# Maxima of the first head's scores: two groups of keys in one VectorE pass, by way of the positive part of their difference

## The reference

```
x = x + L0_xattn(layernorm(x), ctx)      # one head of width 128
x = x + L0_ffn(layernorm(x))             # 8 experts, top 1
x = x + L1_xattn(layernorm(x), ctx)      # 8 heads of width 64, softmax over 6,404 keys
x = x + L1_ffn(layernorm(x))             # 32 experts, top 4 within 4 of 8 groups

# L1_xattn
q = x @ Wq;  k = ctx @ Wk;  v = ctx @ Wv           # 8 heads of 64
attn = softmax(q k^T * 64**-0.5);  out = attn v;  out @ Wo + bo
```

## Time and profile before

| | |
|---|---|
| median of 3 runs | 1416.0 us (1412.88 to 1417.68) |
| the profiled execution | 1413.19 us, of it 1411.4 us span |
| PE / DVE / ACT / POOL busy | 1365.8 / 1017.1 / 803.0 / 969.5 us |
| the first head's maxima, first product to last reduction | 279.64 to 341.42 us of the span |
| first scores of the main loop | 346.65 us |
| granted clock of TensorE from 296.8 to 344.5 us | 0.50 |

### The profile page before, as it was taken

One profiled execution on the slowest core, in us unless ns is written; L12 is line 12 of the kernel. 1 busy time (PEld: TensorE's weight loads), 2 busy tenths in 40 slices (PEclk: granted clock), 3 DMA queues, 4 the chain that ended last, 5 costly groups with the idle time before them and its releaser, 6 DMA issues.

```text
span 1411.4 us, 20075 instructions
## 1 busy us (share of the span) xinstructions
PE 1365.8 (97%) x6259; PEld 786.0 (56%) x6259; DVE 1017.1 (72%) x1420; ACT 803.0 (57%) x1599; POOL 969.5 (69%) x562
## 2 busy tenths in 40 slices
PE   5989998889999999999999999999999999999998
PEld 3877776524455555555545555555555555556665
DVE  8976656598887677777777767677767675876555
ACT  3458887422566656666556665655665655554432
POOL 5001112342889999999999999899999999986110
PEclk9999999976999999999999999999999999999999
DMA  6640000310000200200020020002002000000011
GB/s 175 206 132 18 18 16 10 77 22 0 1 1 1 51 8 1 51 9 0 1 58 1 1 50 9 1 0 59 1 1 48 8 1 1 8 1 24 25 40 36
DMA packets 80537, 41.38 MB, mean 29 GB/s; under 512 B 64301, under 2 KB 72254, under 8 KB 80166
## 3 DMA queue, kind: packets, MB, share of 16 engines
q1 hardware_dynamic: 80454, 40.28, 11.4%
HBM read 26.53 MB, written 13.74 MB: 29 GB/s over the span
## 4 chain that ended last, share of the span: by engine, by line
PE 89%; DVE 6%; DMA 3%; ACT 1%; issue 1%; POOL 0%; SPq 0%; ACTq 0%; POOLq 0%; DVEq 0%
PE ps L1537 26%; PE ps L1524 15%; PE ps L1525 13%; PE ps L1484 9%; PE ps L1471 3%; DMA v_scratch<-v_stage 3%; DVE chunk_max L1054 2%; PE ps L1713 2%; PE ps L1344 2%; PE ps L1345 2%; PE ps L1346 2%; PE ps L1335 2%; PE ps L1333 2%; PE ps L1334 2%; PE ps L1699 1%; PE ps L1701 1%
## 5 line engine op out<-in xcount | busy, mean ns | idle before, releaser
L605 POOL TENSOR_TENSOR psums<-psums,probs 126x1024 f32<-126x1024 f32 (+1 forms) x392 | 821.4, 2095 | 66.0 <-ACT probs L811 11.0
L1054 DVE TENSOR_REDUCE chunk_max<-ps 128x2 f32<-128x1008 f32 (+1 forms) x416 | 473.3, 1182 | 154.2 <-PE ps L1484 153.8
L811 ACT ACTIVATE probs<-ps 126x512 f32<-126x512 f32 (+1 forms) x816 | 412.8, 623 | 270.0 <-PE ps L1525 261.9
L1537 PE MATMUL ps<-probs,v_mem 126*64 126x512 f32 (+1 forms) x1632 | 389.8, 598 | 0.0
L1524 PE MATMUL ps<-q_heads,ring 128*126 128x512 f32 (+1 forms) x816 | 334.2, 410 | 0.6
L1525 PE MATMUL ps<-q_low,ring 128*126 128x512 f32 (+1 forms) x816 | 321.3, 394 | 0.0
L1537 PEld LDWEIGHTS ps<-probs,v_mem 126*64 126x64 f32 (+1 forms) x1632 | 111.6, 136 | 173.4 <-issue 123.0
L1117 DVE TENSOR_TENSOR xn<-xn,probs 126x512 f32<-126x512 f32 x126 | 181.4, 1440 | 21.9 <-ACT probs L811 16.4
L1524 PEld LDWEIGHTS ps<-q_heads,ring 128*126 128x126 f32 (+1 forms) x816 | 151.2, 185 | 80.7 <-issue 44.1
L755 ACT CAST ring<-ps 64x252 fp32r<-64x252 f32 (+1 forms) x356 | 128.3, 360 | 117.3 <-PE ps L1471 114.2
L1484 PE MATMUL ps<-ring,q_heads 64*128 64x504 f32 (+1 forms) x416 | 163.7, 468 | 11.1 <-DVE chunk_max L1054 9.0
(11 more groups left out here) (227 smaller groups left out, 1410.9 us busy)
## 6 DMA issues: line engine op xcount, KB each, us to landing
v_scratch<-v_stage SPq DMA_DIRECT2D x51, 252.0 KB
v_mem<-v_scratch SPq DMA_DIRECT2D x8, 1606.5 KB
ctx_mem<-in_ctx_t SPq DMA_DIRECT2D x3, 803.2 KB, 8.3
vslot<-in_ctx_rows SPq DMA_DIRECT2D x51, 47.2 KB
pair_w<-in_f_pairs SPq DMA_DIRECT2D x17, 128.0 KB, 2.2
xn<-rden_scratch SPq DMA_DIRECT2D x14, 128.0 KB
pair_w<-in_f_pairs SPq DMA_DIRECT2D x17, 65.0 KB, 1.9
x_tok<-in_x SPq DMA_DIRECT2D x1, 512.0 KB, 4.2
```

The costliest lines, as they stand in the source:

```text
L605: pool.tensor_tensor(sums[0:r, 0:width], sums[0:r, 0:width], probs[0:r, n % PROBS, 0:width], ALU.add).then_inc(c_sum, 1)
L811: act.activation(probs[0:r, n % PROBS, cols(half)], ps[0:r, score_bank(t, half), :], ACT.Exp, scale=float(HD) ** -0.5).then_inc(c_exped, 1)
L1054: dve.tensor_reduce(chunk_max[:, h % 2, i:i + 2, c], ps[:, banks[0]:banks[1] + 1, 0:group_tiles(c) * KT], AX, ALU.max).then_inc(c_reduced, 1)
L1537: ins = pe.matmul(ps[half * HD:(half + 1) * HD, B_ACC, :], v_tiles[0:r, h % 2, t, :], probs[0:r, n % PROBS, cols(half)], start=(t == 0), s ...
```

## The change

For two groups of keys with scores a and b, max(a, b) = max(a - b, 0) + b. The first 12 groups are taken two at a time. One such double step `n` (24 in all) covers two groups and two query tiles:

- TensorE accumulates a - b in the two banks of a first pair: two matmuls with the queries on the first group, and two with the negated queries `q_neg` on the second. It puts b alone into a second pair, with two more matmuls. That is six matmuls of 504 columns where two steps had four.
- ScalarE applies Relu to the first pair, 128 x 1008 elements, into a buffer `beyond` (two slots, in memory of `probs` that is not yet in use).
- VectorE runs two `tensor_tensor_reduce`, one for each query tile: 504 elements of b from a bank plus 504 elements of the buffer, and the maximum of the sums into `chunk_max`.

The 13th group keeps the old form: four single steps. So the loop has 28 turns where it had 52. The three pairs of banks are shared out anew: a - b of turn n waits for VectorE's turn n - 2, and b of turn n waits for ScalarE's turn n - 1. The key projections go to ten turns listed in `KEYS_AT`, the second head's queries to turns 16 and 21. `q_neg` is made by VectorE ahead of `q_lo`. The idle matmuls of this stage and of the first lines of the main loop are gone. `row_maxima` of the first head reads 7 columns of `chunk_max` per query tile where it read 13. Semaphores `max_found` and `max_row` are merged into `c_found` and `c_row`.

```diff
+STEPS = TT // 2
+TWO_STEPS = GROUPS_H // 2 * STEPS
+FIRST_STEPS = TWO_STEPS + STEPS
+KEYS_AT = (3, 6, 8, 10, 13, 15, 18, 20, 22, 24)
+QUERIES_FIRST = (16, 21)
...
+        beyond = probs[:, 2:6, 0:GT * KT].rearrange("p (s b) k -> p s b k", s=2)
+        q_neg = q_heads[:, 2, :]
...
@@ ScalarE
-            for g in range(EARLY[2], AHEAD):
-                k_first(g)
-                if g in (EARLY[2] + 1, EARLY[2] + 2):
-                    q_hi(1, g - EARLY[2] - 1, B_AUX)
+            for n in range(FIRST_STEPS):
+                if n < TWO_STEPS:
+                    first = FIRST_PAIRS[2 * n % 3][0]
+                    act.wait_ge(c_max, 4 * n + 2)
+                    if n >= 2:
+                        act.wait_ge(c_reduced, 2 * n - 2)
+                    act.activation(beyond[:, n % 2], ps[:, first:first + 2, 0:GT * KT], ACT.Relu).then_inc(c_over, 1)
+                if n in KEYS_AT:
+                    k_first(EARLY[2] + KEYS_AT.index(n))
+                if n in QUERIES_FIRST:
+                    q_hi(1, QUERIES_FIRST.index(n), B_AUX)
...
@@ VectorE
+            def first_maxima(n):
+                dve.wait_ge(c_max, 4 * n + 4 if n < TWO_STEPS else 2 * (n + TWO_STEPS) + 2)
+                c, i = 2 * (n // STEPS), 2 * (n % STEPS)
+                if n >= TWO_STEPS:
+                    first = FIRST_PAIRS[(n + TWO_STEPS) % 3][0]
+                    dve.tensor_reduce(chunk_max[:, 0, i:i + 2, c], ps[:, first:first + 2, 0:group_tiles(c) * KT], AX,
+                                      ALU.max).then_inc(c_reduced, 1)
+                else:
+                    dve.wait_ge(c_over, n + 1)
+                    for half in range(2):
+                        extra = beyond[:, n % 2, half, :]
+                        dve.tensor_tensor_reduce(out=extra, in0=ps[:, FIRST_PAIRS[(2 * n + 1) % 3][half], 0:GT * KT], in1=extra,
+                                                 scale=1.0, scalar=LOWEST, op0=ALU.add, op1=ALU.max,
+                                                 accum_out=chunk_max[:, 0, i + half, c:c + 1]).then_inc(c_reduced, 1)
+
+            for half in range(2):
+                dve.wait_ge(c_qhi, half + 1)
+                dve.tensor_scalar(q_neg[:, cols(half)], ps[:, FIRST_PAIRS[2][half], :], -1.0, None, ALU.mult).then_inc(c_neg, 1)
...
@@ TensorE
-                if step >= GROUPS_H * STEPS - 6:
-                    pe.wait_ge(c_kfull, AHEAD)
-                    idle(1, FIRST_KP)
-            idle(5, FIRST_KP)
+            first_q = q_heads[:, 0, :], q_low[:, 0, :]
+            for n in range(FIRST_STEPS):
+                c, i = 2 * (n // STEPS), 2 * (n % STEPS)
+                if n < TWO_STEPS:
+                    banks = FIRST_PAIRS[2 * n % 3]
+                    if n == 1:
+                        pe.wait_ge(c_qlo, 2)
+                    if n >= 2:
+                        pe.wait_ge(c_reduced, 2 * n - 2)
+                    first_products(c, i, banks, first_q, True, False)
+                    if n < 2 * STEPS:
+                        pe.wait_ge(c_neg, 1 + i // STEPS)
+                    first_products(c + 1, i, banks, (q_neg, q_neg), False, True)
+                    if n:
+                        pe.wait_ge(c_over, n)
+                    first_products(c + 1, i, FIRST_PAIRS[(2 * n + 1) % 3], first_q, True, True)
+                else:
+                    if n == TWO_STEPS + 1:
+                        pe.wait_ge(c_over, TWO_STEPS)
+                    else:
+                        pe.wait_ge(c_reduced, 2 * TWO_STEPS + {0: -2, 2: 0, 3: 1}[n - TWO_STEPS])
+                    first_products(c, i, FIRST_PAIRS[(n + TWO_STEPS) % 3], first_q, True, True)
...
             row_shift(0, B_AUX)
-            idle(3, FIRST_KP)
+            pe.wait_ge(c_kfull, AHEAD)
...
                         if k and h == 0 and b == 0:
-                            idle(3, B_KEYS)
                             pe.wait_ge(c_shift, 2)
```

More of the change, by code:

```diff
@@ L59 @@
 FIRST_PAIRS, FIRST_KP = ((0, 1), (2, 3), (6, 7)), 4
+GT = 4
+GROUPS_H = -(-TILES // GT)
+STEPS = TT // 2
[3 more added lines that the diff above has]
+QUERIES_FIRST = (16, 21)
+LOWEST = -3.0e38
 EARLY = (3, 3, 5)
 B_LOGITS, B_HIDDEN, B_SPREAD, B_MASK = 0, (1, 2, 3, 6), (5, 1, 2, 3), (7, 0)
[L67 to L68 removed]
 RING = 16
 AHEAD = RING - 1
[L71 removed]
 PROBS = 2 * GT
@@ L1099, in add_last_output @@
                 ins.then_inc(c_x, 1)
+            def first_maxima(n):
[15 more added lines that the diff above has]
+                dve.tensor_scalar(q_neg[:, cols(half)], ps[:, FIRST_PAIRS[2][half], :], -1.0, None, ALU.mult).then_inc(c_neg, 1)
             for half in range(2):
                 q_lo(0, half, FIRST_PAIRS[2][half])
[L1103 to L1106, removed]
+            for n in range(FIRST_STEPS):
+                first_maxima(n)
+                if n in QUERIES_FIRST:
+                    q_lo(1, QUERIES_FIRST.index(n), B_AUX)
             row_maxima(0, GROUPS_H * STEPS)
@@ L1576, in _ @@
                 q_proj(0, half, FIRST_PAIRS[2][half])
[L1577 to L1585, removed]
-                if step % STEPS == 1 and early < AHEAD:
-                    k_proj(early)
-                    early += 1
-                if step in (STEPS + 2, 2 * STEPS + 2):
-                    half = step // STEPS - 1
+            pe.wait_ge(ring_rows, 1)
@@ new lines, in _, with first_products @@
+            pe.wait_ge(c_qhi, 2)
+            pe.wait_ge(c_qlow, 1)
+            def first_products(c, i, banks, q_rows, start, stop):
+                pe.wait_ge(c_khi, c + 1)
+                for half, q in enumerate(q_rows):
+                    rows = slice(half * HD, (half + 1) * HD)
+                    ins = pe.matmul(ps[:, banks[half], 0:group_tiles(c) * KT], q[rows, tile_cols(i + half)],
+                                    ring[rows, c % RING, 0:group_tiles(c), 0, :], start=start, stop=stop)
+                    if stop:
+                        ins.then_inc(c_max, 1)
@@ new lines, in _ @@
+            first_q = q_heads[:, 0, :], q_low[:, 0, :]
+            for n in range(FIRST_STEPS):
+                c, i = 2 * (n // STEPS), 2 * (n % STEPS)
[18 more added lines that the diff above has]
+                    first_products(c, i, FIRST_PAIRS[(n + TWO_STEPS) % 3], first_q, True, True)
+                if n in KEYS_AT:
+                    k_proj(EARLY[2] + KEYS_AT.index(n))
+                if n in QUERIES_FIRST:
+                    half = QUERIES_FIRST.index(n)
```

18 lines of the change are left out of this document (10 added, 8 removed).

## The result

The changed kernel takes **1403.45 us** (median of 4 runs, 1401.96 to 1406.81), where the kernel before, beside it, takes 1415.57 (1412.88 to 1417.68). The ratio is 0.9919, 95% interval 0.9894 to 0.9943: faster, by 12.1 us in the medians where -7.3 was forecast. The profiled execution is the longest of the four: 1406.81 us, span 1405.0. I read both profiles, since they differ by 5.7 us in the same code.

What follows compares the result with a forecast made beforehand. VectorE was taken to bound the first head's maxima stage. Stage -9.4, gap -2.4, main loop's clock +2.0 and stage's clock +2.5 sum to -7.3 us, forecast 1409 us from the median 1416.0, range 1403.5 to 1418.5.

Steps and rivals of the forecast that it cites:

- likeliest case: Whole kernel: clock mostly up, 0.6 to 0.8 us per new VectorE instruction, 1405.5 to 1411.5 us; chance 0.50.
- The stage: First head's maxima: ends at 332.0 instead of 341.42 us, -9.4 at full clock, with +2.5 for spells at 0.50.
- The new VectorE instruction: In each double turn: tensor_tensor_reduce of 504 elements takes 0.70 us, bounds 0.60 and 1.14, so 1.40 a turn.
- the ring: In the double turns: waits through TensorE, ScalarE and VectorE set the pace, 3.55 us for two turns, no engine full.
- The key turns: Ten turns with a key projection: ScalarE's copies make the next Relu 0.475 us late.
- The clock in the stage: First head's maxima: spells at clock 0.50, a fifth of the 12.4 us that a whole stage there costs, +2.5 us.
- The gap: From last reduction to main loop's first scores: 2.83 us instead of 5.23 as the idle matmuls go, -2.4 us.
- The main loop at 0.50: Main loop's start: without the idle matmuls it begins at clock 0.50, costing 1.7 to 3.4 us, taken as +2.0.
- The clock stays up: Rival on TensorE's clock: both clock terms are nothing, -11.8 us, 1404; chance 0.08.
- The clock falls early and stays low: Rival on the stage's clock: at 0.50 from 296.7 us or at once, -1.3 to +2.7 us, 1415 to 1419; chance 0.20.
- Two instructions: Rival on the new VectorE instruction: main pass plus a short one of 0.26, 0.96 us each, -2.1, 1414; chance 0.08.
- As dear as the reduction: Rival on the new VectorE instruction: 1.14 us for 504 elements, +2.7, or likelier +8.1 at clock 0.50, 1424; chance 0.12.

Runs made afterwards that it cites:

- a2: The changed kernel run again, unaltered; 1401.86 us, ratio 0.9927 to the kernel before.
- e5: Kernel of e1 with two idle matmuls more in each of the first 16 turns without a key projection; 1401.39 us, ratio 0.9924.
- e6: Changed kernel with the second copy of each key projection moved from ScalarE to VectorE; 1402.0 us, ratio 0.9934.
- e4: Changed kernel with each turn's Relu split into two instructions, one per bank, with their own signals; 1400.92 us, ratio 0.9918.
- e9: Kernel of e5 with the additional VectorE instruction of e3 in each double turn; 1403.73 us, ratio 0.9925.
- e1: Changed kernel with the idle matmuls of before put back at the stage's end and the main loop's start; 1402.17 us, ratio 0.9916.
- e7: Kernel before with two idle matmuls more behind the products in most steps of the stage; 1436.15 us, ratio 1.0174.
- e8: Kernel before with one or two idle matmuls ahead of the products of every step of the stage; 1412.88 us, ratio 0.9999.
- e3: Changed kernel with one more VectorE instruction, its result unused, in each of the 24 double turns; 1411.08 us, ratio 0.9979.
- e2: Kernel before without the idle matmuls at the stage's end and the main loop's start; 1411.08 us, ratio 0.9988.
- c1: Kernel of e5 plus e4's Relu halves, e6's copy and one idle matmul ahead of the products of the last four turns; 1397.04 us, ratio 0.9878.

## Why the prediction was right, and where its sizes were off

**Direction and bound: right.** The stage was VectorE's, it is shorter by 8.9 and 10.5 us, and that arrives in the total one for one: the rest differs from before by +0.3 and -0.8 us. Forecast 1409 (1403.5 to 1418.5), measured 1403.45, 0.05 below the end of the range and outside the likeliest case's own (1405.5 to 1411.5). From the ratio and the median shown before it is 0.9919 x 1416.0 = 1404.5, just inside. Against a2's profile (-13.4) the forecast of -7.3 was 6.1 us off: 1.9 in the stage at full clock, 1.7 in the clock of the stage, 2.8 in the rest, and -0.3 in the gap.

**The stage: -9.4 + 2.5 = -6.9 forecast, -8.9 and -10.5 measured.** At full clock 52.4 us were forecast, and e5 took 50.5 (2.9 us of it at 0.50, in the last reductions, which kept their spacing).
- *The new VectorE instruction*, 0.70 taken, is the largest of the terms that were mis-sized, 0.11 of the 0.25 us by which the ring was too long. It takes 0.605 from start to start, the lower bound of 0.60. The nearest row was of a plain two-input instruction at 0.69 for 512 elements, a duration of one; it was taken for a spacing. Here the duration is 0.68 too, and the spacing is not.
- *Relu*, 1.05 taken, takes 1.01. The prediction's own walk with 1.29 for VectorE's turn and 1.01 gives 51.2 us, 1.2 of the 1.9 that it was off. Single steps of 0.86 in place of 0.95 are 0.4 of the rest. The remaining 0.3 has no sum of its own, but the hand-overs and products of the ring were 0.10 too long.
- *The key turns*, +0.475 each: two turns with a key took 3.85 against 3.30, so 0.55. Near in size, and right in that the copies delay the next Relu (e6). But the path was not ScalarE's work alone, as the prediction had it: it runs through the key projection too, for which ScalarE waits.
- *The clock in the stage*, +2.5: between e5 and the two profiles it is +2.4 (15.3 us at 0.50) and +0.8 (3.5 us). Right for the profiled execution, too much for most. "Spells rather than 45 us on end" is what came.

**The ring of waits: shown.** e4 shortened a latency and no work, and got 0.43 of 0.42 us. e9 added work to VectorE, paid 2.4 us for 10.4, and its ring adds up too. The forecast of an even turn of 1.775 was wrong in form, as two turns run back to back and then wait; the ring sets what two of them take. And it sets only the pairs without a key projection; the others have the ring of 3.85.

**The gap: -2.4 forecast, -2.1 measured.** Right.

**The main loop at 0.50: +2.0 forecast, +0.3 in the balance.** The main loop did start at 0.50 for 5.5 us, and e1 says that costs up to 2.6, so the term itself was right. The prediction forgot that the rest of the kernel before isn't free of such spells: it had 6.8 us at 0.50 near 1324 us, and the profiled change 3.4 us there. That varies from run to run, and it may well be what hid the term: the rest of the kernel before is 1064.8 us, while e7 and e8, the same code behind the stage with no such spell, have 1061.7.

**The rivals.** *The clock stays up* gives nearly the measured time, but it isn't what happened: the clock fell in both profiles of the changed kernel. That its number is the nearest is luck, made up of the cheaper turns, fewer spells than forecast, and spells of the kernel before. *The clock falls early and stays low* (1415 to 1419) came nowhere near in the changed kernel: it fell in the first turns of the profiled execution and was back 10.2 us later. e3, with 22.6 us of its stage at 0.50, has a stage 3.9 us longer than e9's; a whole stage at 0.50 was not seen. *Two instructions*: they are two. The Trainium skill ("VectorE: DVE Perf Modes", on two Vector instructions with no wait between them) is right that an accumulator output makes a second instruction, and the trace shows it, 0.083 us long; but it starts together with the next pass, so the forecast price of 0.26 was 0 between passes and 0.08 at the end of a turn. *As dear as the reduction*: refuted by 0.605 us.

**What of the gain is whose.** Of the 13.4 us by a2 (12.1 by the medians): the stage 10.5, the gap 2.1, the rest 0.8. Of the stage's 10.5 a full clock could have given the kernel before 2.5 at the most, 0.7 of it also by taking the idle matmuls away; at least 8 are the new form's. e2 says that the idle matmuls alone give 1.7 (0.1 to 3.3 by its interval).

**What stays open:** what makes the clock fall. The same code had 15.3 us of the stage at 0.50 in one execution and 3.5 in another, and e7's stayed low while TensorE counted as busy throughout. And which of c1's edits gives how much.

## What to carry to other kernels

When an engine that bounds a stage can hand half its elements to another engine for one more hand-over, add up the whole ring of waits and not only each engine's work: here no engine was full afterwards, and the pace was 3.30 us for two turns where VectorE had 2.5 us of work. Look for a second ring where other work joins in: with a key projection it was 3.85. Then look at what cuts the latency (halving the instruction that the others wait for) and at what else stands in the slowest engine's queue, and try these together, as three of them alone showed nothing and c1, with a fourth, was 5 us faster. Size a new instruction from the start-to-start spacing of its neighbours, not from their durations, and compare variants at the same granted clock: one of them (e3) was 7 us or more slower, mostly at a lower clock, and looked as if its work had cost it.

## What the runs showed of the hardware that was not expected

- Two VectorE passes over 504 float elements, with one input in PSUM and one in memory and the maximum as a second output, start 0.605 us apart, though each is 0.68 us long; the read of the maximum (0.083 us) runs beside the next pass. The reduction of 1008 elements, one input, takes 1.12 from start to start (1.13 in the earlier trace rows, where the last one counts in full). So the new form reads and sums two inputs for 0.605 us, little more than half a reduction (0.56).
- The clock of TensorE stayed at 0.50 for 71.7 us in e7, in which TensorE counts as busy for 71.5 of 71.5 us (with modelled ends). The Trainium skill ("TensorE: Matmul & The Clock Gate", part 1) says that a busy stretch restores it; if busy is what the profile counts as busy, the trace does not agree. In e8, with idle matmuls of the same kind in other places, it never fell in the stage.
- Run to run the same code had from 3.5 to 15.3 us of the stage at 0.50, and e3's runs spread over 8.8 us, the fastest at the highest granted clock (0.988).
